# A cross network on one core: where three low parts, ten split groups and the table gathers are placed

## The chip, the cores and the metric

The kernel runs on one core of a Trainium2 chip. The metric is the device time of one execution in microseconds. Five engines work from queues of their own, each strictly in its program order, and meet in semaphores: TensorE (PE: matmuls and transposes into PSUM), VectorE (DVE), ScalarE (ACT), GpSimd (POOL) and SyncE (SP, which here only issues DMAs). GpSimd issues the indirect DMAs, called gathers here.

## The reference, cut to what matters

512 examples have 39 ids each; each id picks a 16-wide row of a table. The result is the batch e of shape (512, 39, 16). Three layers of a compressed interaction network follow, then a small dense part:

```
x0 = e; xk = e
for layer in 0, 1, 2:
    z = relu(einsum('bhd,bkd,hks->bsd', x0, xk, W[layer]) + b)   # s = 128
    xk, direct = z[:, :64], z[:, 64:]      # layer 2: all of z is direct
logit = sum over d of all direct parts      # (512, 256)
h = relu([logit, dense_ctx] @ W_top1 + b);  h = relu(h @ W_top2 + b);  y = h @ W_top3
```

All of it is in float32.

## The kernel before, in words

**Tiles.** The batch is cut into 16 chunks of 32 examples; a chunk gives N = 512 columns (16 x 32). For each layer the products x0*xk are formed elementwise as tiles of up to 128 rows by 512 columns, and TensorE multiplies each with a 128-column weight tile and sums into the layer's bank z. Layer 0 has 7 product tiles, in 4 groups (`G0`); layers 1 and 2 have 19 tiles in 10 groups (`G1`; a group is two tiles, the last only one), and a twentieth tile, the stack.

**Whole and split groups.** A whole group is a float32 product in buffer `whole` (4 slots); TensorE multiplies each of its tiles as float32, two instructions a tile in the profile (`whole_group`, L677). A split group (`SPLIT`: group 1 of layer 0, groups 2, 4, 6, 8 of layer 1, groups 2, 5, 8 of layer 2) is a product in `raw` (L601, 2 slots), which ScalarE rounds to its high part in fp32r (`high_part`, L436) and whose low part is raw minus high, made by VectorE (`low_part`, L585) two groups later (`LAG`); high and low have 4 slots. TensorE then runs three fp32r matmuls a tile (`split_group`, L667 to L669). The stack tile holds its high part in rows 0 to 63 and its low part in rows 64 to 127; ScalarE copies it (L443) and GpSimd makes the low half (`stack_part`, L351); TensorE runs two fp32r matmuls (`stacked`, L684 and L685), last in its layer.

**Order.** All queues are written out by hand. `STEPS` is (0,0), (1,0), (0,1), (2,0), (0,2), (1,1), and then for phase p = 1 to 15 the steps (layer 0, chunk p+2), (layer 1, chunk p+1), (layer 2, chunk p), as far as these chunks exist. TensorE and VectorE both follow it, group by group.

**Inputs of a chunk.** GpSimd issues ten gathers a chunk (`gather`, L333) into one of two buffers `emb`; TensorE transposes them (`transposes`, L658 and L660) into the bank `tp`, for chunk p+3 right behind layer 0 of phase p; ScalarE copies them to `xt` (`turned`, L422 and L423), SyncE stores them five times in DRAM (`store`) and loads them back as rotations for layer 0 (`rot`, `rep`) and as broadcasts for layers 1 and 2 (`bc`, in five sections, each released when VectorE has multiplied the old content in layer 2 of two chunks before). ScalarE's queue in a phase is: high of layer 0, layer 2's output, first high of layer 1, `turned(p+3)`, the other highs of layer 1, its stack part, layer 0's output, the highs of layer 2 with layer 1's outputs between.

**GpSimd's queue.** Before the phases it issues 40 gathers, then works through first folds and stack parts with chunks 4 and 5 gathered between. In phase p: the ten gathers of chunk p+4 and a wait until they have landed, the fold of layer 2's chunk p-1 (`fold`, four additions that sum over d), the stack part of layer 1, two folds, the stack part of layer 2. `own_done` before such a part waits for GpSimd's own earlier results.

Of the kernel before, what the change touches and what calls it, by code (L numbers as in the profile page):

```python
# [6 lines left out]
PART = 128  # L7
# [32 lines left out]
SPLIT = {0: (1,), 1: (2, 4, 6, 8), 2: (2, 5, 8)}  # L40
GROUPS = {0: G0, 1: G1, 2: G1}
WHOLE_SLOTS = 4
RAW_SLOTS = 2
PART_SLOTS = 4
LAG = 2
SECTION = 4
SECTIONS = T1 // SECTION
# [13 lines left out]

def whole_tiles(layer):
    return [t for g in range(GROUPS[layer]) if g not in SPLIT[layer] for t in tiles_of(layer, g)]


def split_tiles(layer):
    return [t for g in SPLIT[layer] for t in tiles_of(layer, g)]


def tower(nc, A, fields, out):  # L70
# [4 lines left out]
    with ExitStack() as ctx:  # L75
# [24 lines left out]
        rows_all = sb("rows_all", [PART, CHUNKS, GATHERS], i32)  # L100
# [8 lines left out]
        high = sb("high", [PART, PART_SLOTS, GT, N], fp32r)  # L109
        low = sb("low", [PART, PART_SLOTS, GT, N], fp32r)  # L110
# [6 lines left out]
        dense = sb("dense", [PART, BATCH // PART, DENSE_ROWS])  # L117
# [19 lines left out]
        tp = bank("tp")  # L137
        top = [bank(f"top{n}") for n in range(2)]

        left0 = top[1][0:ROWS0, :]  # L140
        h1_banks = (top[0], top[1], tp, z[0])
# [25 lines left out]
        raw_ready = sem("raw_ready")  # L167
        high_ready = sem("high_ready")
        low_ready = sem("low_ready")
        parts_free = sem("parts_free")  # L170
# [35 lines left out]
        WHOLE_NO = {x: n for n, x in enumerate(x for x in EACH if x[2] not in SPLIT[x[0]])}  # L206
        SPLIT_NO = {x: n for n, x in enumerate(x for x in EACH if x[2] in SPLIT[x[0]])}
# [7 lines left out]
        def wholes_to(layer, c, g):  # L215

            return max(WHOLE_NO[layer, c, h] for h in range(g + 1) if h not in SPLIT[layer]) + 1

        def splits_to(layer, c, g):
            return max(SPLIT_NO[layer, c, h] for h in range(g + 1) if h in SPLIT[layer]) + 1  # L220

        def layer0_read(engine, c):

            engine.wait_ge(whole_ready, wholes_to(0, c, G0 - 1))
            engine.wait_ge(raw_ready, splits_to(0, c, G0 - 1))
# [12 lines left out]
        def _(sp):  # L238
# [30 lines left out]
            def load_broadcasts(c, sections=range(SECTIONS)):  # L269
# [5 lines left out]
                for n in sections:  # L275
                    first, end = SECTION * n, min(LAST, SECTION * (n + 1))
                    if c >= 2:
                        g = (end - 1) // GT
                        sp.wait_ge(whole_ready, wholes_to(2, c - 2, g))
                        if g >= SPLIT[2][0]:  # L280
                            sp.wait_ge(raw_ready, splits_to(2, c - 2, g))
# [528 lines left out]
```

## Time and profile before

| | us |
|---|---|
| median of 3 runs | 673.98 |
| lowest and highest | 672.66, 676.32 |
| the profiled execution, first to last instruction | 674.9 |
| TensorE busy in it | 638.7 |
| VectorE busy | 588.5 |
| GpSimd busy | 314.3 |
| ScalarE busy | 253.3 |

The profile gives the profiled execution's time only as this span. Busy time is a sum over stages with different limits: a start of about 80 us in which TensorE is partly idle, a steady part of equal phases, and an end with the dense layers.

### The profile page before, as it was taken

To read this page: it belongs to the slowest core of one execution; us is meant where nothing else is said; L and a number is where in the kernel's file an instruction comes from. 1 tells how busy PE (TensorE), PEld (TensorE's weight loads), DVE (VectorE), ACT (ScalarE), POOL (GpSimd) and SP (SyncE) were. 2 spreads that over 40 slices of the span, in tenths; PEclk is the share of its full clock that TensorE was granted. 3 is DMA by queue.
4 is the path that set the end of the run, shared out by engine and by line. 5 is a ranking of instruction groups with operands and counts; after the bars stand their busy time and mean duration, and the time that the engine had idled before them with its cause. 6 is when DMAs were issued, how large, how long until landed. Compare 5 with 4: busy or idle time off the path is not lost.

```text
span 674.9 us, 6021 instructions
## 1 busy us (share of the span) xinstructions
PE 638.7 (95%) x1878; PEld 350.3 (52%) x1878; DVE 588.5 (87%) x550; ACT 253.3 (38%) x331; POOL 314.3 (47%) x392
## 2 busy tenths in 40 slices
PE   0777899999999999999999999999999999999998
PEld 0334455555555555555555555555555555555554
DVE  0258598999999999999999999999999999999950
ACT  1122324444444344343344443443433434433322
POOL 6775655436455453546364454536364132122320
PEclk9999699999999999999999999999999999999999
DMA  9689826985757759393857568583948476090200
GB/s 199 171 257 347 236 97 200 286 323 140 259 181 217 246 151 311 73 336 85 317 139 251 194 180 282 149 304 68 341 94 289 155 230 221 13 298 1 68 0 2
DMA packets 126751, 130.12 MB, mean 193 GB/s; under 512 B 60734, under 2 KB 68686, under 8 KB 126719
## 3 DMA queue, kind: packets, MB, share of 16 engines
q1 hardware_dynamic: 117743, 128.23, 59.0%
q0 software_dynamic: 5120, 1.32, 2.1%
q10 hardware_dynamic: 3856, 0.18, 0.4%
q8 instruction: 15, 0.25, 0.1%
q14 instruction: 17, 0.14, 0.1%
HBM read 123.31 MB, written 6.39 MB: 192 GB/s over the span
## 4 chain that ended last, share of the span: by engine, by line
PE 86%; POOL 2%; issue 2%; DMA 2%; DVE 1%; ACT 0%; DVEq 0%; ACTq 0%; POOLq 0%
PE z L677 55%; PE z L667 9%; PE z L668 8%; PE z L669 8%; DMA bc<-fields 2%; POOL emb L333 2%; PE z L684 1%; PE z L685 1%; PE z L750 1%; DVE low L585 1%; PE top L740 1%; DVE raw L601 0%; PE tp L740 0%; PE z L740 0%; PE xk L756 0%
## 5 line engine op out<-in xcount | busy, mean ns | idle before, releaser
L677 PE MATMUL z<-whole,w 128*128 128x512 f32 (+2 forms) x928 | 428.8, 595 | 1.7 <-DVE whole L609 1.0
L677 PEld LDWEIGHTS z<-whole,w 128*128 128x128 f32 (+2 forms) x928 | 175.4, 190 | 157.9 <-issue 140.4
L609 DVE TENSOR_TENSOR whole<-bc,xk 128x1024 f32<-128x1024 f32 (+1 forms) x208 | 231.5, 1134 | 21.5 <-PE z L677 11.6
L436 ACT ACTIVATE high<-raw 128x1024 fp32r<-128x1024 f32 (+1 forms) x128 | 135.4, 1059 | 295.4 <-DVE raw L601 239.0
L333 POOL DMA_INDIRECT emb<-in_tables,rows_all x160 | 168.2, 1052 | 57.4 <-issue 52.4
L585 DVE TENSOR_TENSOR low<-raw,high 128x1024 fp32r<-128x1024 f32 (+1 forms) x128 | 161.5, 1262 | 9.1 <-ACT high L436 9.1
L667 PE MATMUL z<-high,w_high 128*128 128x512 f32 (+1 forms) x256 | 143.7, 561 | 6.6 <-DVE low L585 4.6
L601 DVE TENSOR_TENSOR raw<-bc,xk 128x1024 f32<-128x1024 f32 x112 | 136.0, 1214 | 0.0
L351 POOL TENSOR_TENSOR stack<-stack_raw,stack 64x512 fp32r<-64x512 f32 x32 | 43.6, 1362 | 190.1 <-ACT stack L443 184.0
L668 PE MATMUL z<-high,w_low 128*128 128x512 f32 (+1 forms) x256 | 101.7, 397 | 0.0
L669 PE MATMUL z<-low,w_high 128*128 128x512 f32 (+1 forms) x256 | 101.4, 396 | 0.0
L667 PEld LDWEIGHTS z<-high,w_high 128*128 128x128 f32 (+1 forms) x256 | 48.4, 189 | 58.4 <-DVE low L585 33.2
L362 POOL TENSOR_TENSOR sum<-direct 64x256 f32<-64x256 f32 (+1 forms) x48 | 36.1, 751 | 82.6 <-ACT direct L464 32.0
L668 PEld LDWEIGHTS z<-high,w_low 128*128 128x128 f32 (+1 forms) x256 | 48.6, 190 | 27.5 <-issue 21.2
L669 PEld LDWEIGHTS z<-low,w_high 128*128 128x128 f32 (+1 forms) x256 | 48.4, 189 | 11.8
L609 DVE TENSOR_TENSOR whole<-rot,top 120x1024 f32<-120x1024 f32 (+1 forms) x45 | 45.3, 1036 | 0.4 <-ACT top L429 0.2
L447 ACT ACTIVATE xk<-z,bias 64x512 f32<-64x512 f32 x64 | 41.6, 650 | 7.6 <-issue 6.0
L364 POOL TENSOR_TENSOR sum<-sum 64x128 f32<-64x128 f32 (+1 forms) x48 | 34.3, 714 | 3.8
L684 PE MATMUL z<-stack,w_high 128*128 128x512 f32 x32 | 25.2, 788 | 5.2 <-POOL stack L351 5.2
L443 ACT ACTIVATE stack<-stack_raw 128x512 fp32r<-128x512 f32 x32 | 20.1, 627 | 21.0 <-DVE stack_raw L639 20.5
L475 ACT ACTIVATE direct<-z,bias 128x512 f32<-128x512 f32 x16 | 11.0, 688 | 30.0 <-PE z L685 16.3
L639 DVE TENSOR_TENSOR stack_raw<-bc,xk 128x512 f32<-128x512 f32 x32 | 21.8, 681 | 0.0
(61 smaller groups left out, 198.9 us busy)
## 6 DMA issues: line engine op xcount, KB each, us to landing
bc<-fields SPq DMA_DIRECT2D x64, 1024.0 KB, 6.8
rot<-fields SPq DMA_DIRECT2D x16, 1280.0 KB
bc<-fields SPq DMA_DIRECT2D x16, 768.0 KB
rot<-fields SPq DMA_DIRECT2D x16, 512.0 KB
fields<-xt SPq DMA_DIRECT2D x64, 80.0 KB
bc<-fields SPq DMA_DIRECT2D x32, 128.0 KB
rep<-fields SPq DMA_DIRECT2D x48, 80.0 KB
emb<-in_tables,rows_all POOLq DMA_INDIRECT x160
```

The costliest lines, as they stand in the source:

```text
L333: pool.indirect_dma_start(emb[c % 2][:, j * DIM:(j + 1) * DIM], None, A["tables"], bass.IndirectOffsetOnAxis(rows_all[:, c, j:j + 1], 0)). ...
L351: pool.tensor_tensor(stack[KEEP:PART, :], stack_raw[KEEP:PART, :], stack[KEEP:PART, :], ALU.subtract).then_inc(stack_low, 1)
L362: pool.tensor_tensor(halves[0][part, :], src[part, 0:width], src[part, width:2 * width], ALU.add).then_inc(d_free[layer], 1)
L436: act.activation(high[0:m, k % PART_SLOTS], raw[0:m, k % RAW_SLOTS], ACT.Copy).then_inc(high_ready, 1)
L447: act.activation(xk[layer][half * KEEP:(half + 1) * KEEP, :], z[layer][0:KEEP, :], RELU, bias=bias[0:KEEP, layer:layer + 1]).then_inc(x_re ...
L585: nc.vector.tensor_tensor(low[0:m, k % PART_SLOTS], raw[0:m, k % RAW_SLOTS], high[0:m, k % PART_SLOTS], ALU.subtract).then_inc(low_ready, 1)
L601: nc.vector.tensor_tensor(raw[0:m, k % RAW_SLOTS], left, right, ALU.mult).then_inc(raw_ready, 1)
L609: nc.vector.tensor_tensor(whole[0:rows, n % WHOLE_SLOTS, 0:len(tiles)], left, right, ALU.mult).then_inc(whole_ready, 1)
L667: nc.tensor.matmul(out_z, w_high[0:m, n, :], high[0:m, k % PART_SLOTS, u], start=False, stop=False)
L668: nc.tensor.matmul(out_z, w_low[0:m, n, :], high[0:m, k % PART_SLOTS, u], start=False, stop=False)
L669: ins = nc.tensor.matmul(out_z, w_high[0:m, n, :], low[0:m, k % PART_SLOTS, u], start=False, stop=False)
L677: ins = nc.tensor.matmul(z[layer][:, :], w[layer][0:m, WHOLE_AT[layer, t], :], whole[0:m, k % WHOLE_SLOTS, u], start=(t == 0), stop=(layer ...
```

## The change

It has five parts.

1. `KIND` gives each group a letter: w whole; v split, with product in PSUM (`raw_bank`, one slot of two banks) and low part by VectorE; g split, with product in SBUF (`raw`) and low part by GpSimd. A phase has 7 v groups and 3 g groups. v and g have high and low buffers of their own, 2 slots each.
2. So ten groups a phase are split instead of eight. `TAKEN` is the order in which TensorE takes the groups of a layer; VectorE keeps the ascending order.
3. The transposes go to layer 2's bank z[2] (chunk 3: to z[1]), with waits on both sides. Banks `tp`, `top0` and `top1` become `left` and `raw_bank`.
4. GpSimd: three lows a phase, `low_parts`. The ten gathers of a chunk are issued as three (`EARLY`), with a wait for them, and seven, with a wait, between layer 1's lows and its stack part. Before the phases 30 gathers come first instead of 40.
5. ScalarE takes the highs of layers 1 and 2 in ascending order, two of layer 1 ahead of `turned(p+3)`. `rows_all` and `dense` take over other buffers' space.

```diff
-SPLIT = {0: (1,), 1: (2, 4, 6, 8), 2: (2, 5, 8)}
+KIND = {0: "vwww", 1: "vgwwvgwwvw", 2: "wvwgvwwvww"}
+TAKEN = {0: (1, 0, 2, 3), 1: (2, 0, 1, 3, 6, 4, 5, 7, 9, 8), 2: (0, 2, 1, 5, 4, 3, 6, 8, 7, 9)}
-PART_SLOTS = 4
+PART_SLOTS = {"v": 2, "g": 2}
+EARLY = 3
...
+            def landed_early(c):
+                pool.wait_ge(gathered[c % 2], (c // 2 * GATHERS + EARLY) * 16)
...
+            def low_part(layer, c, i):
+                k, m = NO["g"][layer, c, groups_of(layer, "g")[i]], ROWS[layer]
+                own_done()
+                issued["lows"] += 1
+                pool.wait_ge(high_ready["g"], k + 1)
+                pool.tensor_tensor(low["g"][0:m, k % PART_SLOTS["g"]], raw[0:m, k % RAW_SLOTS], high["g"][0:m, k % PART_SLOTS["g"]], ALU.subtract).then_inc(low_ready["g"], 1)
...
-            for c in range(4):
+            for c in range(3):
                 gather(c)
+            landed(1)
             landed(2)
-            landed(3)
             fold(0, 0)
+            low_parts(1, 0)
             stack_part(1, 0)
             own_done()
-            gather(4)
-            landed(4)
+            gather(3)
+            landed(3)
             fold(1, 0)
+            low_parts(2, 0)
             fold(0, 1)
             stack_part(2, 0)
             own_done()
-            gather(5)
-            landed(5)
+            gather(4, range(EARLY))
+            landed_early(4)
+            low_parts(1, 1)
             stack_part(1, 1)
+            own_done()
+            gather(4, range(EARLY, GATHERS))
+            landed(4)
             fold(0, 2)
             fold(1, 1)
             for p in range(1, CHUNKS + 1):
-                if p > 1 and p + 4 in IN:
+                if p + 4 in IN:
                     own_done()
-                    gather(p + 4)
-                    landed(p + 4)
+                    gather(p + 4, range(EARLY))
+                    landed_early(p + 4)
                 fold(2, p - 1)
                 if p + 1 in IN:
+                    low_parts(1, p + 1)
+                if p + 4 in IN:
+                    own_done()
+                    gather(p + 4, range(EARLY, GATHERS))
+                    landed(p + 4)
+                if p + 1 in IN:
                     stack_part(1, p + 1)
+                if p in IN:
+                    low_parts(2, p)
...
+            def high_parts(layer, c, first=0, end=GATHERS):
+                for g in groups_of(layer, "vg")[first:end]:
+                    kind = KIND[layer][g]
+                    k, m, slots = NO[kind][layer, c, g], ROWS[layer], PART_SLOTS[kind]
+                    src = raw_bank[0:m] if kind == "v" else raw[0:m, k % RAW_SLOTS]
+                    act.wait_ge(raw_ready[kind], k + 1)
+                    if k >= slots:
+                        act.wait_ge(parts_free[kind], k + 1 - slots)
+                    act.activation(high[kind][0:m, k % slots], src, ACT.Copy).then_inc(high_ready[kind], 1)
...
-                    high_part(1, p + 1, SPLIT[1][0])
+                    high_parts(1, p + 1, 0, 2)
                 if p + 3 in IN:
                     turned(p + 3)
                 if p + 1 in IN:
-                    for g in SPLIT[1][1:]:
-                        high_part(1, p + 1, g)
+                    high_parts(1, p + 1, 2)
                     stack_part(1, p + 1)
...
+                if KIND[layer][g] == "v":
+                    k = NO["v"][layer, c, g]
+                    if k:
+                        dve.wait_ge(low_ready["v"], k)
+                    else:
+                        dve.wait_ge(dense_ready, 1)
+                    nc.vector.tensor_tensor(raw_bank[0:m], left, right, ALU.mult).then_inc(raw_ready["v"], 1)
+                    pending.append([-1, (layer, c, g)])
...
+                if c == 3:
+                    pe.wait_ge(x_ready[1], 2)
+                    pe.wait_ge(d_ready[1], 1)
+                elif c > 3:
+                    pe.wait_ge(d_ready[2], c - 3)
+                turn = turn_bank(c)
...
+                if layer == 2:
+                    pe.wait_ge(xt_ready, 2 * min(CHUNKS, c + 4) if c else 6)
```

## Rows read from the trace of the kernel before

**Rows 1.** The page, part 1: busy us (share of span) and instructions.
```profile
PE 638.7 (95%) x1878; PEld 350.3 (52%) x1878; DVE 588.5 (87%) x550; ACT 253.3 (38%) x331; POOL 314.3 (47%) x392
```

**Rows 2.** Two stretches: busy us of PE, PEld, DVE, ACT, POOL; clock, DMA share, GB/s.
```profile
111.00:117.00 6.00, 6.00 (x20) 3.41 (x19) 5.01 (x6) 4.16 (x6) 0.13 (x1) 1.00 1.02 356
...
320.00:360.00 40.00, 40.00 (x122) 22.34 (x120) 39.04 (x38) 16.40 (x21) 20.16 (x28) 1.00 0.64 205
```

**Rows 3.** The chain of waits, pieces in order: start us, us, what.
```profile
157.71 1.72 PE z L677 x4
...
307.23 1.72 PE z L677 x4
...
313.15 3.44 PE z L677 x8
316.58 0.23 PE z L667
316.81 0.24 PE z L668
...
344.59 1.72 PE z L677 x4
```

**Rows 4.** Timeline around the transposes: start us, us, engine, line [idle before, releaser].
```profile
312.11 1.22 DVE L609 TENSOR_TENSOR whole<-bc,xk 128x1024 f32<-128x1024 f32 x1 [0.77 <-PE z L677]
...
312.88 0.27 PE L660 MATMUL tp<-ident,emb 128*32 128x128 f32 x1
...
313.18 0.28 ACT L422 ACTIVATE xt<-tp 128x128 f32<-128x128 f32 x1 [0.75 <-issue]
...
314.49 1.06 ACT L436 ACTIVATE high<-raw 128x1024 fp32r<-128x1024 f32 x1 [0.88 <-DVE raw L601]
```

**Rows 5.** Timeline of VectorE in the same phase.
```profile
322.90 0.68 DVE L639 TENSOR_TENSOR stack_raw<-bc,xk 128x512 f32<-128x512 f32 x1
323.50 1.22 DVE L585 TENSOR_TENSOR low<-raw,high 128x1024 fp32r<-128x1024 f32 x1
324.63 2.35 DVE L609 TENSOR_TENSOR whole<-bc,xk 128x1024 f32<-128x1024 f32 x2
...
330.29 1.60 DVE L585 TENSOR_TENSOR low<-raw,high 128x1024 fp32r<-128x1024 f32 x1
```

**Rows 6.** Timeline of GpSimd in the same phase: gathers, a fold, the stack part.
```profile
316.72 0.94 POOL L333 DMA_INDIRECT emb<-in_tables,rows_all  x1 [0.31 <-issue]
319.27 0.73 POOL L362 TENSOR_TENSOR sum<-direct 128x256 f32<-128x256 f32 x1 [1.61 <-DMA emb<-in_tables,rows_all]
...
321.03 0.25 POOL L368 TENSOR_TENSOR logits<-sum 128x32 f32<-128x32 f32 x1
...
339.99 1.28 POOL L351 TENSOR_TENSOR stack<-stack_raw,stack 64x512 fp32r<-64x512 f32 x1 [7.05 <-ACT stack L443]
342.02 0.96 POOL L333 DMA_INDIRECT emb<-in_tables,rows_all  x1 [0.76 <-issue]
343.29 0.95 POOL L333 DMA_INDIRECT emb<-in_tables,rows_all  x1 [0.30 <-issue]
```

**Rows 7.** Timelines of the start, GpSimd and TensorE: waits for gathers to land.
```profile
15.87 0.95 POOL L333 DMA_INDIRECT emb<-in_tables,rows_all  x1 [0.30 <-issue]
...
19.92 0.47 PE L658 MATMUL tp<-ident,emb 128*128 128x128 f32 x1 [4.97 <-DMA emb<-in_tables,rows_all]
...
117.06 1.27 POOL L351 TENSOR_TENSOR stack<-stack_raw,stack 64x512 fp32r<-64x512 f32 x1 [5.93 <-DMA emb<-in_tables,rows_all]
```

**Rows 8.** Timeline of the start: two gaps of TensorE, GpSimd's 30th gather and first fold.
```profile
39.72 0.50 PE L667 MATMUL z<-high,w_high 120*128 120x512 f32 x1 [3.11 <-DVE low L585]
...
45.80 0.95 POOL L333 DMA_INDIRECT emb<-in_tables,rows_all  x1 [0.30 <-issue]
...
66.34 0.71 POOL L362 TENSOR_TENSOR sum<-direct 64x256 f32<-64x256 f32 x1 [5.24 <-issue]
...
69.69 0.79 PE L684 MATMUL z<-stack,w_high 128*128 128x512 f32 x1 [4.96 <-POOL stack L351]
```

More of the change, by code:

```diff
@@ L59, in tiles_of, with groups_of @@
     return range(GT * g, min(T0 if layer == 0 else T1 - 1, GT * g + GT))
+def groups_of(layer, kind):
+    return [g for g in range(GROUPS[layer]) if KIND[layer][g] in kind]
 def whole_tiles(layer):
-    return [t for g in range(GROUPS[layer]) if g not in SPLIT[layer] for t in tiles_of(layer, g)]
+    return [t for g in groups_of(layer, "w") for t in tiles_of(layer, g)]
 def split_tiles(layer):
-    return [t for g in SPLIT[layer] for t in tiles_of(layer, g)]
+    return [t for g in groups_of(layer, "vg") for t in tiles_of(layer, g)]
 def tower(nc, A, fields, out):
@@ L108, in tower @@
         raw = sb("raw", [PART, RAW_SLOTS, GT, N])
-        high = sb("high", [PART, PART_SLOTS, GT, N], fp32r)
-        low = sb("low", [PART, PART_SLOTS, GT, N], fp32r)
+        high = {k: sb(f"high_{k}", [PART, PART_SLOTS[k], GT, N], fp32r) for k in "vg"}
+        low = {k: sb(f"low_{k}", [PART, PART_SLOTS[k], GT, N], fp32r) for k in "vg"}
         stack_raw = sb("stack_raw", [PART, N])
@@ L136, in tower @@
         xk = [bank(f"xk{n}") for n in range(2)]
[L137 to L141, printed above, removed]
+        left = bank("left")
+        raw_bank = ctx.enter_context(nc.psum_tensor("raw_bank", [PART, GT, N], fp32))
+        left0 = left[0:ROWS0, :]
+        dense_bank = raw_bank[:, 0]
+        h1_banks = (raw_bank[:, 0], left[:, :], raw_bank[:, 1], z[0][:, :])
         ids_in = sem("ids_in")
@@ L213, in tower, with wholes_to, multiplied, turn_bank @@
         WHOLE_AT = {(m, t): n for m in range(3) for n, t in enumerate(whole_tiles(m))}
[L215 to L220, printed above, removed]
+        def wholes_to(layer, c):
+            return max(WHOLE_NO[layer, c, h] for h in groups_of(layer, "w")) + 1
+        def multiplied(engine, layer, c, g):
+            for kind, ready in (("w", whole_ready), ("v", raw_ready["v"]), ("g", raw_ready["g"])):
+                done = [NO[kind][layer, c, h] for h in groups_of(layer, kind) if h <= g]
+                if done:
+                    engine.wait_ge(ready, max(done) + 1)
+        def turn_bank(c):
+            return z[1] if c == 3 else z[2]
         def layer0_read(engine, c):
-            engine.wait_ge(whole_ready, wholes_to(0, c, G0 - 1))
-            engine.wait_ge(raw_ready, splits_to(0, c, G0 - 1))
+            multiplied(engine, 0, c, G0 - 1)
         def store_rows(queue, c, part):
@@ L518, in _ @@
                 if p + 2 in IN:
[L519 to L520 removed]
+                    high_parts(0, p + 2)
                 if p == 1:
```

137 lines of the change are left out of this document (64 added, 73 removed).

## The prediction

> **What bounds the kernel now.** I read the engine totals first, then the busy time by stretch, then the chain of waits, then the timelines of one phase. The totals put TensorE at 95% and VectorE at 87% of a span of 674.9 us [rows 1]; in a stretch of the steady part TensorE is busy 40.00 of 40 us and VectorE 39.04, with GpSimd at 20.16 [rows 2]. The chain of waits is all TensorE there: layer 0 begins at 307.23 and at 344.59, so a phase (one step of each layer) lasts 37.36 us [rows 3]. VectorE's idle time in it is waits for TensorE to free a product buffer, as the 0.77 us in [rows 4]: VectorE runs ahead and is held back. So TensorE is the bound, with VectorE less than a microsecond a phase behind it, and GpSimd is in no one's way: half idle, its only product that TensorE waits for is the stack's low part.
>
> Unit prices. A whole tile is two matmul instructions: 8 of them take 3.44 us, so 0.43 each and 0.86 a tile; a split instruction takes 0.233, three make 0.70 a tile [rows 3]. A phase before: 29 whole tiles 24.9, 16 split tiles 11.2, four stack instructions 0.93, transposes 0.22; sum 37.3, as seen.
>
> **The change, part by part.**
>
> *Ten split groups instead of eight.* Four tiles a phase go from 0.86 to 0.70, minus 0.63 us: TensorE alone would need 37.36 - 0.63 = 36.73 a phase. By that alone the kernel would gain.
>
> *VectorE.* 24 products stay, lows go from 8 to 7. Such an instruction starts 1.13 us after the one before it (323.50 to 324.63), one behind a half-size instruction 0.60 (322.90 to 323.50) [rows 5]. After: 28 x 1.13 + 5 x 0.60 = 34.6 us a phase. What a write into PSUM costs VectorE no row shows. Lower bound 0 (the product takes 1.21 with its second operand already in PSUM), upper bound the slowest 1024-element row, 1.60 instead of 1.22 [rows 5], so +0.4 for 14 instructions, 5.5 us. I take 0, by the rows with a PSUM operand. The single PSUM buffer also makes a v product wait for the low just before it, in two places of layer 2; about 0.1 us each, the 1.22 that it lasts less the 1.13 to the next start. All of it is hidden while TensorE's phase is 37 or more; at the upper bound, 40.1, it would still be below the phase that I forecast.
>
> The lows that today read two SBUF operands disturb GpSimd and are disturbed: the low at 330.29 takes 1.60 instead of 1.22 beside a fold [rows 5]. The Trainium skill (GPSIMD Engine Reference, Key points) says that the two share SBUF interfaces and collide where a VectorE instruction has two SBUF inputs. By it the collisions vanish, since v lows read PSUM; that returns 0.4 us a phase to an engine that is not the bound, and the sum is the same with or without it.
>
> *GpSimd gets three lows.* 256 elements take 0.73 and 512 take 1.28 [rows 6]: 2.1 ns an element, so 1024 elements are 1.28 + 1.09 = 2.4 us. Bounds: 1.28 (as if size were free) and 2 x 1.28 = 2.6. I take 2.4, the line through both rows.
>
> *Gathers dealt out.* One gather follows another after 1.25 us (342.02 to 343.29 is 1.27 with the first); before the first of a batch 0.76 goes by [rows 6]. The whole batch of ten used to be issued while GpSimd had nothing due: it starts at 342.02, behind layer 2's stack. Now three go there, and seven (0.76 + 6 x 1.25 + 0.95 = 9.2 us, then a wait for landing) stand between the second low of layer 1 and layer 1's stack part. GpSimd's queue is in order, so layer 1's stack waits for seven gathers of another chunk.
>
> Is there room? The order of ScalarE's queue ties that chain to TensorE. Call 0 the moment at which TensorE ends the transposes and begins layer 1 (313.15 in the trace). ScalarE copies the transposed block only then (313.18), and the high parts of groups 4 and 5 stand behind these copies. From 0:
> - two copies, to 0.4 (today's high part at 314.49 shows how close it can follow [rows 4]); high of group 4 to 1.4 and of group 5 to 2.5, at 1.06 each;
> - GpSimd's low of group 5, 2.4: to 4.9;
> - 9.2 for the seven gathers: to 14.1;
> - landing. With little else in the queues it is 1.61, the idle time behind 316.72's gather [rows 6]. At 117.06 it was 5.93, with the DMA engines full (share 1.02, 356 GB/s), and at the start 3.1 (last gather ends at 15.87 + 0.95 = 16.8, transposed at 19.92), where the weights' loads run [rows 2, 7]. Here the broadcasts of the next chunk are running: VectorE runs about 7.5 us ahead, ends layer 2's first two groups at about 9.5, and each 1 MB section is released as it goes. I take 3.1, the middle case: to 17.2;
> - the stack's low, 1.28: to 18.5.
>
> TensorE itself needs the stack after 9 whole and 10 split tiles, 9 x 0.86 + 10 x 0.70 = 14.7. It waits 3.8 us, in every phase with gathers. More lead of VectorE does not help, since the chain starts at TensorE's own transposes. With 1.61 the wait is 2.3, with 5.93 it is 6.6. A phase takes 36.73 + 3.8 = 40.5 (39.0 to 43.3). The Trainium skill (DMA: Bandwidth & Descriptors, Anatomy of one DMA) gives a fixed cost of about 2.0 us to a gather of this kind; by it alone the wait would be 2.7, inside my bounds.
>
> *Transposes in layer 2's bank.* They now wait for layer 2's output copy too. ScalarE makes it right after TensorE's layer 2, and layer 0 lies between (5.7 us), so it costs 0; at worst one copy, 0.7 us. Layer 2 in turn waits for the copies out of its bank, done 14 us before. Fewer high and low buffers: the high part of v group n waits for TensorE to end group n-2; ScalarE then waits, but TensorE has 5 us or more of work in hand at each such place; 0, at most the 1.06 of one high part.
>
> *The start.* Before, TensorE waited 4.96 us for layer 1's first stack part (69.69), since GpSimd issued 40 gathers first [rows 8]. Now it issues 30, done at 46.8; landing in a busy queue (5.24, as before the fold at 66.34) takes it to 52, a fold 2.0 (319.27 to 321.28 [rows 6]) to 54, low of group 1 to 56.5. TensorE waits 2.5 there instead and ends the step at 68.5 rather than 70.6; following the same prices through the first steps, it ends step (layer 1, chunk 1) at about 113.8 instead of 118.9 (117.06 + 1.3 + two stack matmuls [rows 7]): 5 us gained. Then the bill. From the end of that stack part (110.4) GpSimd has 0.76 + 8.45 (seven gathers) + 1.6 + two folds 4.2 + 0.75 + 3.5 (three gathers) + 1.6 + fold 2.0 + low 2.4 = 25.2 us until the first low of (layer 1, chunk 2), at 135.5. TensorE wants it at 113.8 + 0.5 + 5.7 + 1.5 (its transposes wait for those gathers) + 3.1 = 124.6: a gap of 11 us. In the same phase the stack comes at 135.5 + 2.4 + 9.2 + 3.1 + 1.3 = 151.5 and phase 1 ends 16 us later, at 167.3; before, it ended at 157.71 [rows 3]. So +9.6 at this point (+8.1 with fast landings, +12.4 with slow ones). A gap of 3.1 us left the clock at full in the trace: after the one before 39.72 [rows 8] the fp32r starts are again 0.23 apart. So the 3.8 us waits should not cost clock; the 11 us gap may, but the wait for the stack behind it takes that up.
>
> *Sum*, against the profiled 674.9: start and phase 1 +9.6; phases 2 to 11 (the ones that still gather) 10 x (40.5 - 37.36) = +31.7; the phases behind, without gathers, three and a half times -0.63, -2.2. 674.9 + 39.1 = 714.0. The median of the runs, 673.98, is 0.9 below the profiled span, so 713.
>
> **Rivals.**
> - *No wait for the stack; TensorE stays the bound* (faster). The phases take 36.73, the start keeps its 5 us: 674 - 5 - 14 x 0.63 = about 660. For it: TensorE and VectorE are the two nearly full engines and both get less work; GpSimd's sum is 34 us in a phase of 36.7. Against it: that sum is in order, and the chain above needs 14.7 and has 17 to 18.5. It decides if GpSimd's low, gathers and landing take under 10.8 us from group 5's high part; the rows give 14.7.
> - *Only phase 1 pays, later phases hide the gathers*: +8 at the start, -0.63 x 10, -2: about 673 to 675, no change.
> - *GpSimd becomes the bound outright*, with lows of 3.5 us or landings near 5.9 for both batches: the phase is 43 to 44, the time 740 to 750. For it: its serial sum is 34 with short landings, 39 to 42 with those. Against it: in the steady part all landings were near 1.6.
> - *VectorE pays 0.4 us for each PSUM access*: 40.1 a phase, by itself 674 + 13 x 2.7 = 709. It hides inside the forecast's phase.
>
> **How the numbers follow.** The forecast (a wait for layer 1's stack of 2.3 to 6.6 us a phase) has 0.70, and its own range is 697 to 745. GpSimd bound 0.12; VectorE bound alone 0.04; no change 0.06; faster 0.08. The range leaves out the upper end of the slow cases and most of the fast one: 692 to 740. About 0.5% is what a measurement tells from no change. Faster by more 0.09, within it 0.04, slower 0.87. Predicted 713.
>
> **What would show it.** Right: TensorE idle before the first stack matmul of layer 1, ended by GpSimd, about 10 times 2 to 7 us; a GpSimd low of 2.4; seven gathers right before layer 1's stack part in each phase; a gap near 11 us at about 124; layer 0 starting every 39 to 43 us until chunk 14, then every 36.7. Wrong: these intervals at 36.7 throughout, or TensorE waiting for low parts on VectorE instead.

## The result: slower by 13.7%, and the profile after

The changed kernel takes 767.48 us (median of 4 runs, 765.13 to 770.82) against 675.15 of the kernel before (672.66 to 678.79): 1.1367 times as long, 95% interval 1.1308 to 1.1425. The direction was as forecast, the size was not: 713 was predicted, with 740 as the upper end. The profiled execution spans 769.0 us (before 674.9), at a mean TensorE clock of 0.936 of full (before 0.992). The ratios below leave out an execution over 1.5% longer than the fastest of the same kernel, as the 695.27 us of `e4_before_dealt`.

Line numbers below are those of the changed kernel. The engine totals of after, the answer to [rows 1]:

```profile
PE 653.5 (85%) x1942; PEld 375.1 (49%) x1942; DVE 569.6 (74%) x534; ACT 275.5 (36%) x363; POOL 395.7 (51%) x440
```

TensorE is no longer full: 85% busy, and more busy time than before for less work. The waits of after, one of GpSimd and one of TensorE (engine, line, who was waited for: total us, times, longest):

```profile
POOL stack L367 <- DMA emb<-in_tables,ids_all: 52.7, 11, 5.3
...
PE z L737 <- POOL stack L367: 63.7, 11, 8.2
```

L737 is the first stack matmul. Eleven waits for GpSimd's stack part, 63.7 us, are by far the largest item of TensorE's; the kernel before had such a wait only once ([rows 8], 4.96). Ahead of each of them GpSimd itself waited for gathers to land, 52.7 us in all. What one of them consists of stands in the chain of waits of the phase whose transposes are at 229.0 (start us, us, what; "issue" ahead of 247.94 is the wait for the seven gathers to land):

```profile
229.09 0.12 PE z L711
...
229.66 0.91 ACT high_v L482
230.56 0.95 ACT high_g L482
231.58 0.09 issue
231.68 2.41 POOL low_g L376
234.22 0.72 issue
234.94 0.96 POOL emb L344
...
242.44 0.94 POOL emb L344
243.38 4.52 issue
247.94 1.27 POOL stack L367
249.25 0.79 PE z L737
250.05 0.43 PE z L738
250.47 5.30 PE z L730 x8
```

The chain starts at TensorE's transposes, runs over ScalarE, a low part on GpSimd, seven gathers, their landing and the stack part, and comes back to TensorE 20.0 us later. TensorE had its other work done at 243.8, 14.6 us after the transposes. And it comes back slow: eight whole matmuls take 5.30 us there, 3.44 in [rows 3]. The stretches (busy us of PE, PEld, DVE, ACT, POOL, then granted clock, DMA share, GB/s) show both causes side by side, full DMA engines (the share can come out a little above 1) while the gathers land and a clock of 0.50, the 1.2 GHz level, after the gap:

```profile
240.00:243.00 3.00, 3.00 (x10) 1.55 (x9) 2.97 (x4) 1.75 (x3) 2.39 (x3) 1.00 1.06 391
243.00:248.00 5.00, 0.82 (x4) 0.34 (x2) 4.97 (x5) 2.24 (x3) 0.44 (x2) 0.93 1.06 369
248.00:253.00 5.00, 3.75 (x6) 2.01 (x7) 0.21 (x1) 0.68 (x1) 4.56 (x4) 0.50 1.05 388
```

VectorE is no part of it. It idles later in the same phase, because TensorE is late (timeline; in brackets the idle time before and who ended it):

```profile
253.93 1.22 DVE L654 TENSOR_TENSOR whole<-bc,xk 128x1024 f32<-128x1024 f32 x1 [5.71 <-PE z L730]
```

**Where the 94.1 us of the span went.** The transposes mark the phases. Those of chunk 5 are at 184.01 (before 163.25): 20.8 us are lost by then. Those ten phases later are at 631.96, so a phase takes 44.8 on average (before 37.36): +74.2. Nine of the ten take 44.3 to 44.8; one takes 47.3, since there GpSimd's first gather of the seven starts 3.54 us after the low instead of 0.86. The ten gaps of TensorE are 5.9 us on average. The end, without gathers, gives 0.9 back.

The start, in three rows of GpSimd and three of TensorE:

```profile
124.94 0.72 POOL L390 TENSOR_TENSOR sum<-direct 64x256 f32<-64x256 f32 x1 [3.88 <-DMA emb<-in_tables,ids_all]
...
136.56 0.72 POOL L390 TENSOR_TENSOR sum<-direct 128x256 f32<-128x256 f32 x1 [3.61 <-DMA emb<-in_tables,ids_all]
...
158.14 1.26 POOL L367 TENSOR_TENSOR stack<-stack_raw,stack 64x512 fp32r<-64x512 f32 x1 [5.27 <-DMA emb<-in_tables,ids_all]
```

```profile
114.42 0.40 PE L737 MATMUL z<-stack,w_high 128*128 128x512 f32 x1
...
141.01 0.80 PE L720 MATMUL z<-high_g,w_high 128*128 128x512 f32 x1 [11.15 <-POOL low_g L376]
...
159.45 0.79 PE L737 MATMUL z<-stack,w_high 128*128 128x512 f32 x1 [4.82 <-POOL stack L367]
```

Three landings of 3.9, 3.6 and 5.3 stand where 1.6, 1.6 and 3.1 were put down, and each of the two gaps of TensorE is followed by a stretch at the lower clock.

### The profile page after: what moved, and what is told of

Read it like the earlier page. It is cut to its first block, busy times and chain, and to the rows that moved or that the text cites. A ratio compares the mean times of both kernels' runs of the same rounds, so it can differ in the third digit from the quotient of the medians.

```text
span 769.0 us, 6461 instructions
## 1 busy us (share of the span) xinstructions
PE 653.5 (85%) x1942; PEld 375.1 (49%) x1942; DVE 569.6 (74%) x534; ACT 275.5 (36%) x363; POOL 395.7 (51%) x440
## 3 DMA queue, kind: packets, MB, share of 16 engines
q0 software_dynamic: 5120, 1.32, 1.8%
## 4 chain that ended last, share of the span: by engine, by line
PE 57%; POOL 17%; issue 14%; ACT 4%; DMA 4%; DVE 3%; POOLq 0%; ACTq 0%; SPq 0%
PE z L730 34%; POOL emb L344 10%; PE z L720 6%; PE z L722 6%; PE z L721 6%; POOL low_g L376 4%; POOL stack L367 2%; DMA emb<-in_tables,ids_all 2%; PE z L737 2%; ACT high_v L482 1%; ACT high_g L482 1%; DVE whole L654 1%; PE z L738 1%; DMA rot<-fields 1%; PE z L807 1%
## 5 line engine op out<-in xcount | busy, mean ns | idle before, releaser
L344 POOL DMA_INDIRECT emb<-in_tables,ids_all x160 | 155.8, 974 | 64.0 <-issue 45.1
L482 ACT ACTIVATE high_v<-raw_bank 128x1024 fp32r<-128x1024 f32 (+1 forms) x112 | 113.9, 1017 | 206.8 <-DVE raw_bank L641 116.7
L623 DVE TENSOR_TENSOR low_v<-raw_bank,high_v 128x1024 fp32r<-128x1024 f32 (+1 forms) x112 | 136.1, 1216 | 36.0 <-ACT high_v L482 35.9
L376 POOL TENSOR_TENSOR low_g<-raw,high_g 128x1024 fp32r<-128x1024 f32 x48 | 113.8, 2371 | 66.0 <-ACT high_g L482 63.0
L720 PE MATMUL z<-high_v,w_high 128*128 128x512 f32 (+1 forms) x224 | 132.4, 591 | 6.6 <-DVE low_v L623 6.4
L641 DVE TENSOR_TENSOR raw_bank<-bc,xk 128x1024 f32<-128x1024 f32 x96 | 117.3, 1222 | 7.8 <-ACT xk L493 6.7
L722 PE MATMUL z<-low_v,w_high 128*128 128x512 f32 (+1 forms) x224 | 88.4, 394 | 0.0
L721 PE MATMUL z<-high_v,w_low 128*128 128x512 f32 (+1 forms) x224 | 88.0, 393 | 0.0
L737 PE MATMUL z<-stack,w_high 128*128 128x512 f32 x32 | 23.4, 731 | 63.7 <-POOL stack L367 63.7
L720 PEld LDWEIGHTS z<-high_v,w_high 128*128 128x128 f32 (+1 forms) x224 | 42.5, 190 | 41.3 <-issue 25.4
L647 DVE TENSOR_TENSOR raw<-bc,xk 128x1024 f32<-128x1024 f32 x48 | 58.0, 1208 | 0.0
L482 ACT ACTIVATE high_g<-raw 128x1024 fp32r<-128x1024 f32 x48 | 50.6, 1055 | 18.4 <-DVE raw L647 17.7
L720 PE MATMUL z<-high_g,w_high 128*128 128x512 f32 x96 | 38.5, 401 | 11.9 <-POOL low_g L376 11.9
```

What stands on the lines that cost most here:

```text
L344: pool.indirect_dma_start(emb[c % 2][:, j * DIM:(j + 1) * DIM], None, A["tables"], bass.IndirectOffsetOnAxis(rows_all[:, c, j:j + 1], 0)). ...
L376: pool.tensor_tensor(low["g"][0:m, k % PART_SLOTS["g"]], raw[0:m, k % RAW_SLOTS], high["g"][0:m, k % PART_SLOTS["g"]], ALU.subtract).then_ ...
L482: act.activation(high[kind][0:m, k % slots], src, ACT.Copy).then_inc(high_ready[kind], 1)
L623: nc.vector.tensor_tensor(low["v"][0:m, k % slots], raw_bank[0:m], high["v"][0:m, k % slots], ALU.subtract).then_inc(low_ready["v"], 1)
L641: nc.vector.tensor_tensor(raw_bank[0:m], left, right, ALU.mult).then_inc(raw_ready["v"], 1)
L647: nc.vector.tensor_tensor(raw[0:m, k % RAW_SLOTS], left, right, ALU.mult).then_inc(raw_ready["g"], 1)
```

## The experiments

Two theories met at the start. The first: in-order GpSimd holds layer 1's stack back behind seven gathers, and the excess over the forecast is longer landings plus TensorE's lower clock. Its rival: the excess comes from GpSimd's lows or from the PSUM product as such, and the place of the gathers matters little. Times are medians; each ratio is against the kernel before, run on the same chip. What each expectation calls its theory and rival stands in it. In the profiles of some experiments the line numbers stand a few lines further on, since lines were added.

**Seven gathers behind the stack part** (`e2_seven_behind`):

```diff
+                if p + 1 in IN:
+                    stack_part(1, p + 1)
                 if p + 4 in IN:
                     own_done()
                     gather(p + 4, range(EARLY, GATHERS))
                     landed(p + 4)
-                if p + 1 in IN:
-                    stack_part(1, p + 1)
```

> The changed kernel with one edit on GpSimd: the seven gathers and their landing wait stand behind layer 1's stack part instead of ahead of it. Theory (the in-order chain through the seven gathers delays the stack part): TensorE's wait before layer 1's first stack matmul goes from 5.4 us to nearly 0, its slow clock behind that wait goes with it, and a phase falls from 44.4 to 36.7 to 38.5 us (the low of layer 2's group 3 comes at about 24.3 us of the phase, wanted at 23.1). Total 767 - 10 x (6 to 7.7) = 690 to 707. Rival (the phases are long because VectorE or TensorE pay for PSUM products, split groups or the shared bank): nothing but the place of seven gathers changes, so the time stays within 1% of 767.

705.56 us, ratio 1.043 (1.0387 to 1.0472). One swap gives 62 of the 92 us back, with the lows, PSUM products and ten split groups untouched: the rival falls. The total is inside the forecast of 690 to 707, at its upper end. The wait moves to the next in GpSimd's queue, layer 2's low part; the waits and the timelines of GpSimd and of TensorE:

```profile
PE z L720 <- POOL low_g L376: 30.8, 12, 9.8
```

```profile
275.29 2.36 POOL L376 TENSOR_TENSOR low_g<-raw,high_g 128x1024 fp32r<-128x1024 f32 x1 [4.91 <-DMA emb<-in_tables,ids_all]
```

```profile
277.71 0.50 PE L720 MATMUL z<-high_g,w_high 128*128 128x512 f32 x1 [1.98 <-POOL low_g L376]
279.45 5.01 PE L730 MATMUL z<-whole,w 128*128 128x512 f32 x8
```

A gap of under 2 us, and again eight whole matmuls at 5.01 instead of 3.44. But not every such gap does this. Of the ten phases with gathers, three have a gap of 1.98 to 2.00 us and the lower clock behind it and take 40.4; one has a gap of 4.26, also with the lower clock, and takes 43.9; the six others have gaps of 1.58 to 1.86, keep the clock at 1.00 and take 38.3 to 38.5.

**The gap filled** (`e3_fill_gap`): the clock priced by itself.

```diff
+            def fill(c):
+                pe.wait_ge(x_ready[0], 2 * (c + 2))
+                for _ in range(FILL):   # FILL = 5
+                    nc.tensor.matmul(z[0][:, :], ident[:, :], w[1][:, 0:N // OUT, :], start=True, stop=True)
...
+                if layer == 1 and 2 <= c <= 12:
+                    fill(c)
                 if layer:
                     stacked(layer, c)
```

> The changed kernel with five float32 matmuls of 128x512, whose result nobody reads, into layer 0's free bank just before layer 1's stack matmuls of chunks 2 to 12, behind a wait that this bank has been read. They fill TensorE's idle time of 5.4 us and leave the stack part as late as it is. Theory (of 7.8 us lost in a phase 5.4 are the wait and 2.3 to 2.5 the low clock behind it): the granted clock stays at full, the phase falls from 44.4 to 42.0 to 42.5, the total by 20 to 25 us to 742 to 747. Rival (the clock's dip costs nothing since other waits would take the time): 767 or slower by what the fillers overrun.

745.82 us, ratio 1.1023 (1.0977 to 1.1069): 21.7 us below the change, though TensorE does more work. The filler ends 0.58 us before the stack matmul, the clock stays at 1.00, and the eight matmuls are back at 3.59:

```profile
245.32 0.50 PE L738 MATMUL z<-stack,w_high 128*128 128x512 f32 x1 [0.58 <-POOL stack L368]
245.66 0.39 PE L739 MATMUL z<-stack,w_low 128*128 128x512 f32 x1
245.89 3.59 PE L731 MATMUL z<-whole,w 128*128 128x512 f32 x8
```

```profile
243.00:248.00 5.00, 4.42 (x12) 1.87 (x11) 1.22 (x2) 0.68 (x1) 3.63 (x3) 1.00 1.05 382
```

The usual phase is 42.4 to 42.9 instead of 44.3 to 44.8. So the lower clock costs about 2.0 us in each of the eleven steps that were filled, 21.7 in all, which the prediction put at nothing.

**Five early gathers instead of three** (`e6_early5`), five left ahead of the stack:

```diff
-EARLY = 3
+EARLY = 5
```

> The changed kernel with five early gathers and five ahead of the stack part, instead of three and seven. Theory: the chain loses 2 x 1.25 = 2.5 us, TensorE's wait falls from 5.4 to 2.9, which is short enough to leave the clock at full, as the 3.1 us gap in the kernel before did; so a phase falls by 2.5 + 2.3 = 4.8 to about 39.6, total about 719 (the start gains up to 2.5 more). If the clock did not depend on the length of the gap, 2.5 a phase, 742. Rival (landing, not the number of gathers, sets the chain: fewer gathers land no earlier): 760 or more.

737.52 us, ratio 1.0904 (1.086 to 1.0948). The 719 of the theory is missed by 18 us; the time is 5 below the 742 foreseen if the clock does not care how long the gap is. Two gathers fewer are 2.5 us less in the chain, the landing is no shorter (5.12), and a gap of 3.51 is followed by the lower clock just as one of 5.44 is, as are all ten gaps of 3.09 to 3.64 in these phases:

```profile
280.17 0.79 PE L737 MATMUL z<-stack,w_high 128*128 128x512 f32 x1 [3.51 <-POOL stack L367]
```

```profile
280.00:285.00 5.00, 4.83 (x7) 2.51 (x8) 1.19 (x2) 0.68 (x1) 4.32 (x7) 0.50 1.05 388
```

**Who lengthens the landing?** Two cuts of the broadcast loads that run meanwhile. First `e9_small_bc`, with fewer rows:

```diff
-                    sp.dma_start(bc[b][:, first:end, :], src).then_inc(bc_in[b][n], 16)
+                    # from chunk 5: source and target cut to 16 of 128 rows
+                    sp.dma_start(bc[b][0:16, first:end, :], src).then_inc(bc_in[b][n], 16)
```

> The changed kernel with the five large broadcast loads of chunks 5 to 15 cut to 16 of 128 rows (the other rows keep old values, so part of the products of layers 1 and 2 is computed from the wrong chunk). Theory (gathers behind layer 1's lows land late, 4.5 to 5.3 us after the last one, because the broadcast loads fill the DMA engines at that moment): the landing falls to about 1.6 us, TensorE's wait to about 2.4, a phase from 44.4 to 41.4 if the clock still dips and to 39.1 if it does not; the total to 705 to 735. Rival (the landing time belongs to this kind of DMA after a batch, whatever else moves): landing stays at 4.5 or more and the total at 760 or more.

767.72 us (2 runs, 760.14 and 775.30; the trace is of the longer one). These are the rival's numbers. But the cut did not take away the load that it was to take away: the DMA share was still 1.04 while the gathers were issued (236 to 243). It fell to 0.39, with 53 GB/s, in 243 to 250, and even so the gathers landed 6.63 us after the last one; over the phases the landing took from 2.3 to 7.3 us. So neither the mean DMA share nor the GB/s at the moment of landing gives its length, and the test does not decide whether the loads do. The second cut, `e13_quarter_loads`, keeps all 128 rows and loads one tile of each section instead of all:

```diff
-                    sp.dma_start(bc[b][:, first:end, :], src).then_inc(bc_in[b][n], 16)
+                    # from chunk 5
+                    sp.dma_start(bc[b][:, first:first + 1, :], src).then_inc(bc_in[b][n], 16)
...
-                    sp.dma_start(rot[:, first:last, :], src).then_inc(arrived, 16)
+                    sp.dma_start(rot[:, first:first + 1, :], src).then_inc(arrived, 16)
```

> The changed kernel in which, from chunk 5 on, each large load of broadcasts and rotations brings only its first tile of 128 rows x 2 KB (the other tiles keep old values, so most products are computed from wrong chunks). Packets and rows per load stay as they are, the bytes fall to about a quarter; the earlier cut to 16 rows kept the engines at a share of 0.5 to 1.2 while it moved few bytes. Theory (gathers land late because the loads in the queues are ahead of them): landing behind the seven gathers falls from 4.5 to 5.3 to 1.6 to 2.5 us, TensorE's wait from 5.4 to 2.5 to 3.5, a phase to 39 to 42, total 705 to 740. Rival (the landing time does not come from other traffic): landing stays above 4 us, total above 755.

731.45 us, ratio 1.0846 (1.0811 to 1.0881), 36 below the change. The waits, a landing, and the stretch around it:

```profile
POOL stack L375 <- DMA emb<-in_tables,ids_all: 21.2, 11, 3.8
```

```profile
239.97 1.26 POOL L375 TENSOR_TENSOR stack<-stack_raw,stack 64x512 fp32r<-64x512 f32 x1 [1.63 <-DMA emb<-in_tables,ids_all]
```

```profile
236.00:243.00 7.00, 4.48 (x14) 2.46 (x13) 6.93 (x7) 4.67 (x6) 4.79 (x4) 0.93 0.32 82
```

With a DMA share of 0.32 instead of 1.06 the landing is 1.63, near the steady value of [rows 6]; in all phases from the third on it is 1.43 to 1.75. (In the first two it is 3.84; only loads of chunk 5 and later are cut.) So the loads lengthen it, as full loads of 128 rows; by what path is open, and `e9` shows that few bytes alone do not make it short. TensorE's gap is then 2.52, and the clock still falls: the same eight matmuls take 5.29. The next rows, two phases of this run with gaps as good as equal, price the clock alone:

```profile
322.64 0.51 PE L745 MATMUL z<-stack,w_high 128*128 128x512 f32 x1 [2.32 <-POOL stack L375]
...
323.22 5.29 PE L738 MATMUL z<-whole,w 128*128 128x512 f32 x8
...
363.36 0.50 PE L745 MATMUL z<-stack,w_high 128*128 128x512 f32 x1 [2.33 <-POOL stack L375]
...
363.93 3.60 PE L738 MATMUL z<-whole,w 128*128 128x512 f32 x8
```

The first phase has the lower clock and takes 40.7, the second keeps it at 1.00 and takes 39.0. The Trainium skill (DMA: Bandwidth & Descriptors, Latency and other measured facts) gives memory access as short on average and much longer under load; the landings of these two kernels agree in direction, 4.4 to 5.3 us beside 370 GB/s and 1.6 beside 82; the 6.63 of `e9` beside 53 does not, and no run here shows memory access by itself.

**Only the dealt gathers, in the kernel before** (`e4_before_dealt`): three, the fold, seven, then the stack part; no GpSimd low, no PSUM product.

```diff
-                    gather(p + 4)
-                    landed(p + 4)
+                    gather(p + 4, range(3))       # and a wait for them
                 fold(2, p - 1)
+                if p > 1 and p + 4 in IN:
+                    own_done()
+                    gather(p + 4, range(3, GATHERS))
+                    landed(p + 4)
```

> The kernel before with one part of the change alone: from phase 2 on, the ten gathers are issued as three, the fold of layer 2, and seven right ahead of layer 1's stack part. Theory (the seven gathers hurt only because GpSimd's lows, tied to ScalarE's copies of the transposed block, hold them back until about 5 us into layer 1): here they can start 3 us before layer 1 and end with landing by 11 us, wanted at 14.7, so the time stays at 674 to 677. Rival (seven gathers ahead of the stack part are too late by themselves): 20 us or more slower.

685.72 us (683.41 to 695.27), ratio 1.0131 (1.0081 to 1.0181). I expected no more than 677; the three shorter executions, 683.4 to 687.6, miss that by 6 to 11 us. I had reckoned that without the low of 2.4 the chain would just fit. The trace shows two things that were not in it, but it is of the longest execution, 695.27, so it cannot say how much of the loss in the other three they make (timelines of GpSimd and of TensorE in a phase of 41):

```profile
249.27 1.84 POOL L333 DMA_INDIRECT emb<-in_tables,rows_all  x1 [0.30 <-issue]
...
260.04 1.27 POOL L351 TENSOR_TENSOR stack<-stack_raw,stack 64x512 fp32r<-64x512 f32 x1 [4.28 <-DMA emb<-in_tables,rows_all]
```

```profile
261.36 0.50 PE L688 MATMUL z<-stack,w_high 128*128 128x512 f32 x1 [1.86 <-POOL stack L351]
261.70 0.40 PE L689 MATMUL z<-stack,w_low 128*128 128x512 f32 x1
261.93 5.29 PE L681 MATMUL z<-whole,w 128*128 128x512 f32 x8
```

At 246.18, 249.27 and 252.67 gathers are stretched from 0.95 to 1.54 to 1.85 while VectorE makes lows from two SBUF operands, as they all are in this kernel; and behind this gap of 1.86 us the clock falls. It does not fall behind every gap of that size: in the same trace those of 1.02 to 1.56 us kept it, and so did the 1.86 at 555.49 in `e2`. Dealing the gathers out ahead of the stack costs about 9 us by itself, 1.3%, of the 92. What makes the other 83 out of it was not taken apart: this kernel also lacks GpSimd's low of 2.4 us with its tie to ScalarE's copies, and the new start, in which 20.8 are lost.

**Five early, five behind the stack** (`e5_five_behind`: both edits, of `e6` and of `e2`):

```diff
-EARLY = 3
+EARLY = 5
...
+                    stack_part(1, p + 1)
...
                     gather(p + 4, range(EARLY, GATHERS))
                     landed(p + 4)
-                    stack_part(1, p + 1)
```

> The changed kernel with five early gathers and the other five behind layer 1's stack part. Theory: the batch behind the stack part ends 2.5 us earlier than with seven there, so the low of layer 2's group 3 comes in time and the phases go to 36.7 to 37.5 us; total 690 minus up to 15, so 678 to 692, and what remains above the kernel before lies in the start (two batches and three folds ahead of the first low of layer 1, chunk 2). Rival (GpSimd's queue is full: its serial sum with loaded landings is 37 us a phase, and moving gathers from one batch to the other only moves the wait, now to the first low of layer 1): phases of 38 us or more, 700 or more.

689.48 us, ratio 1.0192 (1.0135 to 1.025). The steady phases are 36.4 to 38.0, 37.2 on average, so they cost no more than before. All of the rest is the start, 14.7 us longer than before up to chunk 5's transposes, with one wait of 14.1 us for the first low of (layer 1, chunk 2).

**The start dealt anew** in three kernels. `e7_nine_start` takes layer 2's g group back to whole, which leaves nine split groups and two GpSimd lows, issues chunk 4 as 7 + 3 and chunk 5 whole in phase 1, and in later phases three early and seven behind the stack part (its edits of `TAKEN` and inside the phases are left out below); `e10_before_start` gives the kernel before the order of the changed start.

```diff
-KIND = {0: "vwww", 1: "vgwwvgwwvw", 2: "wvwgvwwvww"}
+KIND = {0: "vwww", 1: "vgwwvgwwvw", 2: "wvwwvwwvww"}
...
-            gather(4, range(EARLY))
-            landed_early(4)
+            gather(4, range(7))
+            part_landed(4, 7)
             low_parts(1, 1)
             stack_part(1, 1)
             own_done()
-            gather(4, range(EARLY, GATHERS))
+            gather(4, range(7, GATHERS))
             landed(4)
-            fold(0, 2)
-            fold(1, 1)
```

> The changed kernel with three edits: layer 2's group 3 whole again (nine split groups, two lows on GpSimd), the seven gathers behind layer 1's stack part, and the start re-dealt (seven and three gathers of chunk 4; chunk 5 whole behind the stack part of phase 1; layer 1's lows ahead of the folds there). Theory: TensorE's phase is 36.73 + 0.32 = 37.05, nothing waits, and the start is 4 to 9 us shorter than before: total 674 - 4 - (4 to 9) = 661 to 668, faster than both kernels. Rival (the clock dips or waits come from PSUM products and the shared bank): 680 or more.

677.94 us, ratio 1.003 (1.0 to 1.006): 661 to 668 was expected, a miss by 10 us. The steady phases are 36.75 (37.05 foreseen); phase 1 is what failed. Its ten gathers stand ahead of layer 2's stack and are followed by a landing and two folds, so TensorE waits there:

```profile
160.44 0.80 PE L743 MATMUL z<-stack,w_high 128*128 128x512 f32 x1 [6.65 <-POOL stack L367]
```

```diff
-            for c in range(4):
+            for c in range(3):
                 gather(c)
+            landed(1)
             landed(2)
-            landed(3)
             fold(0, 0)
             stack_part(1, 0)
             own_done()
-            gather(4)
-            landed(4)
+            gather(3)
+            landed(3)
...
-                if p > 1 and p + 4 in IN:
+                if p + 4 in IN:
```

> The kernel before with the start of the change alone: 30 gathers first, chunk 3 behind the first stack part, chunk 4 behind the second, chunk 5 in phase 1. Theory (TensorE's 4.96 us wait for the first stack part comes from the 40 gathers ahead of it, and the low clock behind it): 3 to 6 us faster, 669 to 673. Rival (another wait, on the first broadcast loads or on the gathers of chunk 3, takes its place): no change.

680.13 us, ratio 1.0071 (1.003 to 1.0111): a miss. The early wait of [rows 8] goes, and one of 4.86 us for the stack part comes at 143.36; chunk 5's transposes are at 167.67, 4.4 later than before. The new start is no gain by itself: the gathers that it puts off come back where GpSimd has more to do.

**One order for the phase, nine splits** (`e11_nine_order`) and ten (`e12_ten_order`). GpSimd's order is written so that each landing falls into a wait that is there anyway (the conditions for the first and last chunks are left out here; the start is that of `e7`):

```diff
             for p in range(1, CHUNKS + 1):
+                low_part(1, p + 1, 0)
+                fold(0, p + 1)
+                low_part(1, p + 1, 1)
+                fold(1, p)
+                fold(2, p - 1)
+                stack_part(1, p + 1)
+                gather(p + 4, range(7))      # e12: low_parts(2, p) first, then range(6)
+                part_landed(p + 4, 7)
+                stack_part(2, p)
+                gather(p + 4, range(7, GATHERS))
+                landed(p + 4)
```

> The kernel with nine split groups and a new order on GpSimd. In a phase: low of group 1, fold, low of group 5, two folds, layer 1's stack part, seven gathers of chunk p+4, layer 2's stack part, three gathers of the same chunk. Theory: with landings of 4.9 and 1.5 us GpSimd is done with each part 2 us before TensorE wants it, phases stay at 36.75 as in the run with nine split groups, and the 6.7 us wait in phase 1 goes (the ten gathers there no longer stand ahead of layer 2's stack part); total 678 - 7 to 9 = 668 to 671, 1% faster than the kernel before. Rival (another wait in phase 1 or 2 takes its place, such as transposes waiting for the last three gathers): 675 or more.

666.75 us (663.93 to 673.15, 8 runs), ratio 0.9902 (0.9868 to 0.9935): 1% faster than the kernel before, and a little below the 668 to 671 expected. A phase takes 36.74, and over 37 us TensorE is never idle. GpSimd's timeline shows why the seven gathers now cost nothing: what ends the wait behind them is ScalarE's high part of layer 2's stack, not the DMA.

```profile
232.00:269.00 37.00, 37.00 (x116) 21.46 (x115) 35.28 (x34) 15.71 (x21) 22.30 (x27) 1.00 0.67 211
```

```profile
242.57 1.31 POOL L367 TENSOR_TENSOR stack<-stack_raw,stack 64x512 fp32r<-64x512 f32 x1
244.64 0.95 POOL L344 DMA_INDIRECT emb<-in_tables,ids_all  x1 [0.76 <-POOL stack L367]
...
252.14 0.94 POOL L344 DMA_INDIRECT emb<-in_tables,ids_all  x1 [0.30 <-issue]
258.31 1.27 POOL L367 TENSOR_TENSOR stack<-stack_raw,stack 64x512 fp32r<-64x512 f32 x1 [5.22 <-ACT stack L490]
```

> The same order with all ten split groups of the change: the low of layer 2's group 3 stands behind layer 1's stack part, then six gathers, layer 2's stack part, four gathers. Theory (GpSimd's serial sum is 34 us plus landings of 4.9 and 1.5, minus what overlaps with nothing: 37 us a phase, equal to TensorE's 36.4): phases of 36.8 to 38, total 668 to 685. Rival (it fits, since 0.3 us less matmul time in a phase counts): 665 or less.

671.48 us (12 runs), ratio 0.9955 (0.9934 to 0.9976). With the third low the landing is exposed again on GpSimd (11 waits for it, 55.7 us in all), phases vary from 36.7 to 37.5, and the tenth split group earns nothing. Both orders beat the kernel before with PSUM products and GpSimd lows in them, which confirms that neither costs time by itself.

Not tried: taking away only the wait for the seven gathers to land while they stay ahead of the stack part.

## Why the prediction was right in direction and wrong in size

- *VectorE.* Right. A v product takes 1.222 us with its result in PSUM, a low that reads PSUM 1.215: the upper bound of 0.4 us an access is refuted. VectorE never was the bound. By form (line, engine, operation, count | busy us, mean ns | idle before):

```profile
L641 DVE TENSOR_TENSOR raw_bank<-bc,xk 128x1024 f32<-128x1024 f32 x96 | 117.3, 1222 | 7.8 <-ACT xk L493 6.7
...
L623 DVE TENSOR_TENSOR low_v<-raw_bank,high_v 128x1024 fp32r<-128x1024 f32 x96 | 116.6, 1215 | 28.3 <-ACT high_v L482 28.1
...
L376 POOL TENSOR_TENSOR low_g<-raw,high_g 128x1024 fp32r<-128x1024 f32 x48 | 113.8, 2371 | 66.0 <-ACT high_g L482 63.0 <-POOL low_g L376 0.2
```

- *GpSimd's low.* Right: 2.37 against 2.4, the line through the two sizes of [rows 6].
- *The chain to the last gather.* Right: 14.1 forecast, 243.38 - 229.21 = 14.2 measured; the low ends at 4.9, as forecast. TensorE is ready for the stack after 14.6 (14.7 forecast).
- *Landing: mis-sized.* "I take 3.1, the middle case." It is 4.4 to 5.3 beside full DMA engines; the right row was the one at 117.06, 5.93 at a DMA share of 1.02 [rows 2, 7], since the same kind of load was named in the same sentence. With it the usual gap is 5.4 and not 3.8; the ten gaps average 5.9 (with the one late start of the gathers, a gap of 8.17), 21 us more in ten phases than forecast. The landings stayed inside the prediction's own bounds of 1.61 to 5.93 us.
- *"So the 3.8 us waits should not cost clock": failed.* The prediction put this term at nothing and gave it no bound. It makes about 22 us in the ten phases and more at the start. Neither step took the time out of the range alone: with the gap filled the time is 745.8, still above 740 and just above the forecast's own 697 to 745; with short landings and the clock still falling it is 731.5, inside. The step rested on one gap of 3.1 us at 39.72. The other gap of [rows 8], 4.96 us, stood beside it with its answer: the matmul behind it lasts 0.79 where the one at 39.72 lasts 0.50, and the stretch behind it in the trace of before reads

```profile
69.50:74.50 5.00, 4.81 (x8) 2.08 (x8) 0.41 (x1) 3.35 (x6) 2.05 (x3) 0.50 1.05 387
```

  a clock of 0.50. In the runs after, all gaps of TensorE from 3.0 us up in the phases with gathers were followed by a stretch at the lower level; of those between 1.8 and 2.7 some were (2.52, 1.98, 1.86) and some were not (2.33 in `e13`, 1.86 in `e2`, 2.63 at 153.40 in `e12`). Length alone does not decide it, so the one gap at 39.72 could not carry the step. Filling the gap gave 2.0 us a phase, 21.7 in all. The usual steady phase adds up: 36.7 of work, 5.4 of gap and 2.5 of matmuls at the lower clock (5.30 - 3.44 for the eight, 1.22 - 0.57 for the two stack matmuls, whose length at full clock the filled gap shows) are 44.6; 44.5 is the usual phase, and 40.5 had been forecast. The whole adds up too: 714.0 forecast for the span, 42.5 more in the ten phases (gaps 21, the rest the lower clock), 11.2 more at the start and 1.3 less given back at the end make the 769.0 measured. The layer 0 intervals of "39 to 43 us" were 44.3 to 47.3.
- *The start.* The gain up to (layer 1, chunk 1) came, as 4.0 us and not 5: its stack matmul is at 114.42, 118.39 before (113.8 was forecast for its end). The gap of 11 us came too (11.15). The rest is +20.8 where about 10 was forecast: GpSimd's stack part of that step ended at 111.9 and not 110.4 (1.5), landings 3.88 and 3.61 instead of 1.6 each (4.3), 5.27 instead of 3.1 (2.2), and the way from the stack matmul at 159.45 to the next layer 0 at 178.3 took 18.9 and not 16 (2.9), with the clock at 0.50 in 160 to 165. "The wait for the stack behind it takes that up" held for the clock loss behind the 11 us gap, which the wait for the stack hid; but that wait of 4.82 us brought a second clock loss, which nothing hid.
- *Ten splits, transposes in layer 2's bank.* No cost, as forecast: the phases of `e5` run from 36.4, those of `e12` from 36.7. The end gave back 0.9 and not 2.2. Nine splits were 37.05 by the price list (37.36 - 0.31) and took 36.74; why is open.
- *The rivals.* "GpSimd becomes the bound outright" (740 to 750, chance 0.12) was nearest in time, and it named landings near 5.9. Its mechanism is not what happened: GpSimd is 51% busy, and in every phase the chain starts anew at TensorE's transposes, with GpSimd waiting for ScalarE's high parts (63.0 us before the lows, in the rows above). Landings near 5.9 were argued down by the steady rows of before, where the batch stood in another place of the phase, beside other loads. A landing belongs to its moment and not to the kernel.

## What to carry to other kernels

Before an instruction is put into an in-order queue, list what stands behind it and when that is due; gathers belong where the queue's next wait ends later than their landing, which here, with the start dealt anew, turned 1.137 into 0.996 with the same ten split groups, and into 0.990 with nine. Once a wait is gone, look for the next one in the same queue. Take a landing's price from the row with the same DMA load, not from a middle value. Price any gap of TensorE of about 2 us or more twice, the gap and the matmuls that may come at the lower clock behind it, and look at every gap in the trace for what the first matmuls after it take.

## What the hardware showed unexpectedly

- TensorE's granted clock fell from 2.4 to 1.2 GHz (1.00 to 0.50) around gaps as short as 1.98 us (`e2`; 1.86 in the longest execution of `e4`), while it outlived one of 3.11 at 39.72 of the kernel before. Two gaps of 2.32 and 2.33 us in one run, `e13`, had different outcomes: 1.7 us lost behind the first, nothing behind the second. Gaps of 11.15 and of 3.51 us cost about the same 2 to 3 us afterwards; a longer gap did not cost more there.
- Gathers of 8 KB (1.32 MB in 160) land in 1.6 us with the DMA engines at 0.32 (`e13`) and in 4.4 to 5.3 with them at 1.06 (the changed kernel). Yet one landing took 6.63 us, most of it beside 53 GB/s at a share of 0.39, behind loads cut to 16 rows (`e9`).
- A gather's issue on GpSimd stretched from 0.95 to 1.54 to 1.85 us beside VectorE lows that read two SBUF operands (`e4`); with one operand in PSUM, in the changed kernel, it stayed at 0.94 to 0.97 from 45 us on.
